# Attention in two rounds of visits per batch, with five pairs of tiles prepared ahead instead of nine and four output projections at the end instead of eight

## The reference

```
q, k, v = x@Wq, x@Wk, x@Wv            # 16 heads of width 16
node_probs = softmax(x@Wr over K=4)   # 4 nodes per head and row
expected_pos = cumsum(node_probs over rows) - node_probs
cos_w, sin_w = interpolated rotary tables at expected_pos, weighted by node_probs
q_r, k_r = rotate(q), rotate(k)
scores = q_r k_r^T * scale + log(node_probs_i . node_probs_j + 1e-8), causal
out = softmax(scores) v ; x = x + out@Wo
```

## Time and profile before

| | us |
|---|---|
| median of 3 runs | 3009.42 (3005.66 to 3010.15) |
| the profiled execution | 3003.83 |
| its span, first to last instruction | 3002.0 |
| PE busy | 2526.9 (84%) |
| DVE busy | 1667.9 (56%) |
| ACT busy | 1669.4 (56%) |
| POOL busy | 545.4 (18%) |

### The profile page before, as it was taken

One profiled execution on the slowest core, in us unless ns is written; L12 is line 12 of the kernel. 1 busy time (PEld: TensorE's weight loads), 2 busy tenths in 40 slices (PEclk: granted clock), 3 DMA queues, 4 the chain that ended last, 5 costly groups with the idle time before them and its releaser, 6 DMA issues. The chain is left out here.

```text
span 3002.0 us, 106279 instructions
## 1 busy us (share of the span) xinstructions
PE 2526.9 (84%) x48012; PEld 1984.4 (66%) x48012; DVE 1667.9 (56%) x3557; ACT 1669.4 (56%) x2102; POOL 545.4 (18%) x529
## 2 busy tenths in 40 slices
PE   7277734546999999999999999999999999862786
PEld 4155412225888888888888888888888888741554
DVE  7633148886676667676676656766422222267331
ACT  6021124335777777777777777777766666460221
POOL 1068710001010100010010100001000000010787
PEclk9588866667999999999999999999999999985888
DMA  6445501001111111112111111211111111261555
GB/s 224 138 89 99 78 26 42 28 28 50 46 51 40 51 47 54 48 46 68 50 59 46 55 60 50 59 45 53 56 49 42 44 42 40 68 231 22 99 97 74
DMA packets 170130, 194.78 MB, mean 65 GB/s; under 512 B 33296, under 2 KB 149024, under 8 KB 169504
## 3 DMA queue, kind: packets, MB, share of 16 engines
q1 hardware_dynamic: 143904, 153.01, 16.6%
q0 software_dynamic: 24576, 34.10, 7.2%
q10 hardware_dynamic: 1152, 0.26, 0.0%
HBM read 119.10 MB, written 76.02 MB: 65 GB/s over the span
## 5 line engine op out<-in xcount | busy, mean ns | idle before, releaser
L1090 ACT ACTIVATE at_ew<-at_ring 128x1024 f32<-128x1024 f32 (+2 forms) x1280 | 1116.8, 899 | 402.0 <-PE at_ring L1465 287.1
L1488 PEld LDWEIGHTS at_mix<-at_val,at_ew 128*64 128x64 f32 x34816 | 1207.6, 137 | 157.4 <-issue 20.0
L1488 PE MATMUL at_mix<-at_val,at_ew 128*64 128x68 f32 x34816 | 1255.6, 223 | 3.9 <-issue 3.2
L1465 PE MATMUL at_ring<-at_qT,at_kT 98*64 98x512 bf16 (+3 forms) x5120 | 729.1, 350 | 17.9 <-DMA at_kT<-k_parts 12.7
L1337 DVE TENSOR_TENSOR at_mixed<-at_mix,at_prob 128x272 f32<-128x272 f32 x256 | 112.4, 439 | 572.2 <-PE at_mix L1488 554.8
L1465 PEld LDWEIGHTS at_ring<-at_qT,at_kT 98*64 98x64 bf16 x5120 | 263.2, 111 | 82.1 <-issue 27.3
L1035 POOL TENSOR_TENSOR at_val<-at_prob,at_eps_t 128x64 f32<-128x64 f32 x64 | 19.6, 306 | 1228.2 <-PE at_mix L1488 1228.2
L328 POOL DMA_INDIRECT out_dram<-ffn_xn,ffn_idx_all x128 | 223.1, 1743 | 60.8 <-issue 36.0
L1540 PE MATMUL at_side<-at_w_all,at_turned 128*64 128x512 f32 (+1 forms) x1024 | 210.0, 558 | 14.8 <-ACT at_vo L1110 7.8
L392 ACT ACTIVATE ffn_w1T<-ffn_pair 128x512 f32<-128x512 f32 x16 | 9.6, 598 | 372.1 <-PE ffn_pair L677 342.9
L1469 PE MATMUL at_ring<-at_late_kq,at_ident_b 128*64 128x128 bf16 x2048 | 204.3, 220 | 0.5 <-issue 0.5
(11 more groups left out here) (227 smaller groups left out, 2864.7 us busy)
## 6 DMA issues: line engine op xcount, KB each, us to landing
table<-ffn_xn SPq DMA_DIRECT2D x32, 512.0 KB, 6.3
q_parts<-at_parts SPq DMA_DIRECT2D x64, 192.0 KB, 2.4
k_parts<-at_parts SPq DMA_DIRECT2D x64, 192.0 KB, 2.6
at_qT<-q_parts SPq DMA_DIRECT2D x64, 192.0 KB
at_kT<-k_parts SPq DMA_DIRECT2D x64, 192.0 KB
ffn_front<-in_L_attn_x_dram SPq DMA_DIRECT2D x16, 512.0 KB, 5.4
ffn_w_in<-in_L_ffn_w_dram SPq DMA_DIRECT2D x32, 256.0 KB, 3.0
at_xin<-out_dram SPq DMA_DIRECT2D x32, 256.0 KB, 3.4
```

The costliest lines, as they stand in the source:

```text
L1090: act.activation(ew[u % NE_BUF][:, 0:w], ring[u % 2][:, 0:w], ACT.Exp).then_inc(s["exp_ready"], 1)
L1465: lastm = pe.matmul(ring[u % 2][h:h + HALF, at:at + w], kT[q][:, (j + n) * P + h:(j + n) * P + h + HALF], qT[q][:, c * 512 + t * P:(c + 1) ...
L1488: lastm = pe.matmul(mix[c % 2][h:h + HALF, t * K * VW:(t + 1) * K * VW], ew[u % NE_BUF][:, col + h:col + h + HALF], val[q][:, j + n, :, :] ...
```

## The change

The heads of a batch are visited twice. In the first round (`phase` (0, 1)) all 16 heads do query blocks 0 and 1, 6 units a visit; in the second (`phase` (2, 3)) they do blocks 2 and 3, 14 units a visit. There are 128 visits instead of 64 heads, still 1280 units. `load_head`, `weigh_values` and `begin_visit` (the former `begin_head`) are now executed for each visit; a visit of the first round loads columns 0 to 1023 of q and k, one of the second round columns 1024 to 2047 of q and all 2048 of k. The wait is the same rule, with the visit in the place of the head. The first round needs only 4 pairs of its batch, so `LEAD` is 5. The turns are no longer two heads: four short ones of 24 units (the first round of batch 0) and then 30 of 40 units. A post is given to the first free turn after its block is done for all heads, and 28 fit (`TAIL` = 28). Values are kept in another batch's slot of `vo`.

```diff
-    LEAD = PB + 1
-    TAIL = TP - PB
+    PHASES = [(0, 1), (2, 3)]
+    LEAD = 5
+    SHORT, LONG = 24, 40
+    N_SHORT = 4
+    TAIL = TP - 4
...
+    visits = [(b * H + h, phase) for b in range(B) for phase in PHASES for h in range(H)]
...
+    def pairs_for(v):
+
+        i, phase = visits[v]
+        return i // H * PB + (phase[-1] + 1) * CH // G
...
+        def schedule(lead, first_visit, unit, last_projections):
 
             for t in range(LEAD):
+                lead(t, t - 1 if t else None)
+            first_visit()
+            for m, (start, size) in enumerate(turns):
+                for at in range(min(size, U - start)):
+                    unit(start + at, at, size == SHORT, new_of(m), fin_of(m), posts.get(m))
             last_projections()
...
+                def load_head(v):
+                    q, (i, phase) = v % 2, visits[v]
+                    if v >= 2:
+                        sp.wait_ge(s["av_done"], first_unit[v - 1] + PRIME_E)
+                    sp.wait_ge(s["part_stored"], pairs_for(v) * 64)
+                    q0, k1 = phase[0] * 512, (phase[-1] + 1) * 512
                     for (dst, src, rows) in ((qT, q_parts, Q_ROWS), (kT, k_parts, K_ROWS)):
                         for at, n, first in rows:
                             if src is q_parts:
+                                part, s0 = src[i, :, first:first + n, q0:k1].rearrange("d a s -> a d s"), q0
                             else:
+                                part, s0 = src[i, :, first, 0:k1].unsqueeze(0).to_broadcast([n, HD, k1]), 0
+                            sp.dma_start(dst[q][at * HD:(at + n) * HD, s0:k1], part).then_inc(qk_loaded[q], 16)
...
+                def unit(u, at, short, new, fin, post):
+                    if u + 2 in first_unit and u + 2 < U:
+                        load_shift(first_unit.index(u + 2))
+                    if u - 1 in first_unit:
+                        v = first_unit.index(u - 1) + 1
+                        if 1 < v < V:
+                            load_head(v)
+                    if at == 0:
+                        load_x(new)
+                    if at == 2 and post is not None:
+                        load_residual(post, 0)
+                    if at == (18 if short else 24):
+                        store_parts(fin)
+                    if at == 16 and post is not None:
                         store_output(post, 0)
...
+                SHORT_AT = (1, 4, None, None, 9, 10, 13, 16, 19, 21)
+                LONG_AT = (1, 3, 7, 9, 13, 15, 17, 20, 24, BURST)
...
+                def unit(u, at, short, new, fin, post):
+                    if u + 2 < U:
+                        if u + 2 in first_unit:
+                            begin_visit(first_unit.index(u + 2))
+                        scores(u + 2)
+                    weigh_until(u - 1)
+                    where = SHORT_AT if short else LONG_AT
+                    if at in where:
+                        steps(new, fin, post)[where.index(at)]()
+                    if not short and (at == 0 or at >= BURST):
+                        weigh_until(u)
```

More of the change, by code:

```diff
@@ L776, in width, with new_of, fin_of @@
         return at + (CH - t) * P
-    last_of = [max(u for u in range(NU) if units[u][0] == c) for c in range(NC)]
-    pieces = [(t, a, min(1024, (t + 1) * P - a)) for t in range(TB) for a in range(0, (t + 1) * P, 1024)]
-    NP = len(pieces)
+    NP = max(len(p) for p in pieces)
+    NT = max(tiles_of(v)[1] for v in range(V))
+    turns, at = [], 0
+    while at < U:
+        m = len(turns)
+        turns.append((at, SHORT if m < N_SHORT else LONG))
+        at += turns[-1][1]
+    posts, free = {}, 0
+    for post in range(TAIL):
+        done = max(u for u in end_of if block_of[u] < blocks_until(post))
+        m = max(free, min(n for n, (start, size) in enumerate(turns) if start > done))
+        posts[m], free = post, m + 1
+    assert len(posts) == TAIL and max(posts) < len(turns)
+    def new_of(m):
+        return LEAD + m if LEAD + m < TP else None
+    def fin_of(m):
+        return LEAD + m - 1 if LEAD + m - 1 < TP else None
     with ExitStack() as ctx:
@@ L1426, in run @@
                         statistics(new + 1)
[L1427 to L1428 removed]
+                    if step == 8 and fin is not None:
                         bound(fin)
[L1430 to L1432 removed]
+                    if step == 9 and new is not None:
                         node_products(new)
[L1434 to L1435 removed]
@@ new lines, in lead @@
+                def lead(new, fin):
+                    (turn_inputs, project_values, turn_outputs, output, sums_before, turn_rotated, take_high_off,
+                     take_middle_off, turn_squares, project_qk) = steps(new, fin, early=True)
+                    for step in (turn_inputs, project_values, project_qk, sums_before, turn_rotated, take_high_off,
+                                 take_middle_off, turn_squares):
+                        step()
+                SHORT_AT = (1, 4, None, None, 9, 10, 13, 16, 19, 21)
@@ new lines, in _, with weigh_until, unit @@
+                LONG_AT = (1, 3, 7, 9, 13, 15, 17, 20, 24, BURST)
+                weighed = [0]
+                def weigh_until(u):
+                    while weighed[0] <= u:
+                        weighted(weighed[0])
+                        weighed[0] += 1
+                def unit(u, at, short, new, fin, post):
+                    if u + 2 < U:
[3 more added lines that the diff above has]
+                    weigh_until(u - 1)
+                    where = SHORT_AT if short else LONG_AT
+                    if at in where:
+                        steps(new, fin, post)[where.index(at)]()
+                    if not short and (at == 0 or at >= BURST):
+                        weigh_until(u)
```

425 lines of the change are left out of this document (209 added, 216 removed).

## The result

The changed kernel takes 3265.81 us in the median (3260.39 to 3269.82, 4 runs) beside 3008.69 for the kernel before: a ratio of 1.0855, 95% interval 1.0836 to 1.0874. The forecast was 3182 us, slower, in a range from 3040 to 3330. Direction and range held; the loss is 257 us where 173 were forecast.

What follows compares the result with a forecast made beforehand. PE's work sets the pace in the 32 turns; preparation is a chain between engines. -107 + 248 + 34 - 65 + 15 + 12 + 35 = +172 on 3003.8 gives 3176, plus 5.6 for the median: 3182 us, range 3040 to 3330.

Steps and rivals of the forecast that it cites:

- What is taken away: Outside the turns: four pairs less ahead, 134 us; four closing posts less, 13; first load's wait, some 6 less.
- The load: First-round q and k load: half the bytes in each row, landing 7.7 us after SP's first issue.
- The period: First-round visit: landing 7.7, signals 0.15 and PE work 3.4 make 11.25 us where the multiply trails, against 6.7.
- the visits that don't trail: First-round visits from unit 26 on in a long turn: period 10.25 us, 20 of the 59 loads.
- the 63 counted: Loads costed as stalling PE: 59 issued inside first-round visits, 248 us, and four first second-round visits, 34 us.
- The clock: PE at half clock behind the first-round load wait in one visit in three, 1.7 us each: +35 us.
- The rival of a half clock throughout: PE stays at half clock through the first rounds, each visit's 3.4 us doubled: 3347 us, chance 0.12.
- The four pairs in short turns: Four pairs' preparation moved into turns at 9.6 us each, 38 us; a short turn's excess covered by the load stall.
- the faster rival: The loads never make PE wait: 2914 us, chance 0.10.
- DVE's piece: DVE's products and sums for a pair, in one piece between mixes; PE waiting on it would show the prediction wrong.
- 248 + 34 - 65 + 15 + 12: First-round load stalls, first second-round visits, PE side work hidden in stalls, SP's queue delays, added branches, in us.
- The turns' lengths named ahead: First-round turns near 45 to 50 us (short) and 75 to 80 (long), where PE's work is 37 and 56.

Runs made afterwards that it cites:

- spread: Changed kernel with each load's rows reordered, dimension first, so each of six DMAs has outer size 16: 3078.08 us, ratio 1.0246 to the kernel before.
- filler: Changed kernel with 40 useless PE matmuls before the load wait of a visit that follows a first-round visit: 3216.95 us, ratio 1.0708 to the kernel before.
- both: Changed kernel with loads released once visit v-2's scores are formed and rows reordered to outer size 16: 3034.67 us, ratio 1.0117 to the kernel before.
- the two remedies: Changed kernel with the earlier load release and the loads spread by outer size 16, together: 3034.67 us, ratio 1.0117 to the kernel before.
- the cut DVE piece: The two remedies' kernel with DVE's node sums taken five units later (two in a short turn): 3013.16 us, ratio 1.0049 to the kernel before.

## Why the forecast was right, and where its sizes were off

**What is taken away** was sized well: 135.6 us ahead of the turns (forecast 140) and 17.1 behind them (13).

**The load** was read rightly from the residual's landing and the stretches. Issue to score was put at 7.7 + 0.15; the median is 8.6. Of these 0.7 us, the run without the branch shows 0.4 to be the branch; the rest I can't divide. That the number of rows doesn't set the landing is shown by `spread`, and that few engines do fits it. (Where the prediction gives engines 0 and 1 "66 of the 192 rows", it is 66 each.)

**The period** as a chain of landing and three multiplies was right: releasing the load earlier took 222 us away. (The 10.25 us of the visits that don't trail should be 10.35 by its own terms, 2 us in all.) The total wait came out near the forecast with some luck: each load took 0.7 us longer, but only 55 of the 63 counted made PE wait. In batch 0 it was 10, not 15; besides, PE waited 36 us for ACT there.

**The clock** is the mis-sized term: "one visit in three, at 1.7 us: +35". PE's busy time in the turns rose by 162 us, of which the moved steps are 46 by the forecast's own prices. Some 116 us are left, three times the 35. Releasing the loads earlier gave 79 of them back, the filler 88. The idling was as forecast, 3.7 us in the median and up to 6.6 where 4.5 stood; what failed was the guess how often this is enough: behind 39 of the 55 waits the multiplies ran at half clock, not behind a third. The rival of a half clock throughout, with 200 us, was too much: the clock averages 0.85 in the first rounds. The measured 3266 us lies midway between the forecast's 3182 and this rival's 3347. The Trainium skill, TensorE: Matmul & The Clock Gate, Part 1, has the half rate as the state after idling; the row at 1331.10 and `filler` agree.

**The four pairs in short turns** were put at 4 x 9.6 = 38 us and "covered by the stall below". With the load's stall gone (`both`) they cost 220.9 - 107 = 114 us, 28 each, against 33.4 ahead of the turns. This step failed as an argument, and the load's stall hid it only in part: I compared sums of busy time (41 us of DVE) with PE's work and left out the chain between engines, which had been the reading of the preparation itself. The engine that makes PE wait there is ACT, which the sum did not name: 38.6 us in the changed kernel, 36.4 of them in batch 0's first round. It also is why the faster rival could not have come true: almost without load waits this kernel takes 3034.7, not 2914.

**DVE's piece** was named as a thing that could make PE wait, and costed at nothing; PE's wait for DVE's mixes is 18 us in the changed kernel and 59 once the loads are on time. By the forecast's own list this was a sign of being wrong.

**Together.** The turns took 94 us more than the forecast's 2215. PE's busy time is 81 us of this (116 of clock where 35 stood). Its idle time grew by 257 us where 248 + 34 - 65 + 15 + 12 = 244 were forecast: loads 209, less than forecast, and 57 for ACT and DVE, which had stood at nothing. So the number fell into the range with the main mechanism right, its largest side effect three times too small, and two waits left out. The turns' lengths named ahead were too short: the short ones took 63 us on average (45 to 50), the first-round long ones 95 (75 to 80).

## What to carry to other kernels

Splitting work into more, smaller visits multiplies whatever each visit loads, and shrinks the time that hides it: compare the landing with the work between the release of the buffer and its first use, not with the mean DMA share. Let the last reader of a buffer release it, and give a DMA an outer size that spreads over the engines. When a chain of steps is moved beside other work, look for its longest piece on every engine that the other work also needs, not only at the sums of busy time: in turns of 24 units PE waited 41 us for ACT, in turns of 32 and 40 about 4. With three turns of 32, six pairs ahead, the two remedies and the cut DVE piece, two rounds gain 0.3% (0.14 to 0.43%).

## What the runs showed of the hardware that was not expected

PE came back at half clock behind most of its waits of 2.6 to 6.6 us between pieces of dense work (39 of 55 with over 1.7 us for 28 matmuls that take 0.99), and two waits of 3.50 and 3.53 us ended at different clocks. 2.4 us of useless matmuls inside the waits kept the full clock and made the kernel 49 us faster, though they delayed PE where it had nothing to wait for. A branch in PE's program just behind a wait, with the code that it jumps over, cost 0.4 us there. Putting 16 in the place of 3, 2 and 1 as the outer size of six DMAs of 32 to 96 KB brought the first score 2.7 us forward and the kernel's time down by 188 us.
